# A 32-batch GRU recurrence on one core: in its last five steps, r and h_n are laid ahead of z, and z goes to a bank of its own

## The chip, the cores and the metric

The kernel runs on one core of a Trainium2 chip. The metric is the device time of one execution in microseconds; less is better. Engines: PE (TensorE) multiplies matrices into PSUM, ACT (ScalarE) applies functions, DVE (VectorE) does elementwise work, reductions and 32x32 transpositions, POOL (GpSimd) does little here, and SP (SyncE) issues the DMAs.

## What is computed

A GRU with batch B = 32, T = 64 steps and D = 512 runs over `x`, then a block attention with a layer norm over its output. All values are float32. Cut to what matters here:

```
def cell(h, x):                       # 64 times, each on the h of the one before
    i_r, i_z, i_n = split(x @ W_ih + b_ih)
    h_r, h_z, h_n = split(h @ W_hh + b_hh)
    r = sigmoid(i_r + h_r)
    z = sigmoid(i_z + h_z)
    n = tanh(i_n + r * h_n)
    return (1 - z) * n + z * h
x = x + GRU(x)
# attention over 8 blocks of 8 steps: keys = block sums @ Wk.T, RMS-normed, dotted
# with a query, softmax; attended = weighted block sums; proj = attended @ Wo.T
out = x + layernorm(x + proj) * gamma + beta
```

Step t needs the state of step t-1, so the 64 steps are one chain. z is needed only for the last line of the cell, r and h_n for the tanh.

## The kernel before, in words

**Layout.** State and gates stand in "recurrence layout": partition 32 j + b holds quarter j (128 columns of 512) of batch row b. So each of r, z, n is a tile of 128x128. For h @ W_hh the state is transposed in 32x32 blocks (`turned`), and for each of 4 chunks k of the contraction four matmuls, one for each quarter j, run beside each other on four column strips of the array; each has a stationary tile of 128x32 and moves 384 columns: r, z and h_n of that quarter (L648, 16 matmuls a step; the profile counts 32, two passes each). They add onto what ACT has put into the bank `gates_ps` before: the bias of h_n (`seed_n`, L417) and i_r, i_z (`seed_rz`, L426).

**A step** t = i*8 + s: PE's 16 matmuls (`gates_ready`); ACT's sigmoid over r and z in one instruction of 256 columns (L493); DVE's product r * h_n (L937, `rh_ready`); DVE adds i_n in two parts, 32 and 96 columns (L944); ACT takes tanh of each (L502); DVE forms (z - 1) * n (L862), subtracts it from z * h (L939, L945 make `zh`; L869) and turns the new state (L875) in three parts of 32, 32 and 64 columns; PE's group k = 0 waits for the first part, k = 1 for the second, k = 2 and 3 for the third (`ht_ready`). ACT seeds h_n's columns after L937 and those of r and z after the tanhs.

**Between the steps** each engine runs other work in program order, behind its part of the step. Up to step 58 PE computes x @ W_ih for later steps (L616). In the last five steps, t = 59 to 63 (s = 3 to 7 of the last block), that has run out. PE has there: two of four key matmuls of 512 columns in each of steps 59 to 62 (L630; `keys(0, ..)` in 59 and 60, `keys(1, ..)` in 61 and 62), a mask matmul behind them in step 59 (L658), the first four blocks' scores in step 61 (L662), the tokens' sums of squares in step 62 (L670). ACT has `add_beta` (L453), `centre_wo` (L471), `square_keys` (L433), which waits for the keys, the statistics of a token tile (L439, L442) and `move_s2` (L479). DVE has the sum x + h in transposed layout (L881, step 59), after which SP sends the state out as `h_tok` (L257, 4 DMAs), token centring (L898), the keys' dot products, the early scores (L1036, L1038, step 60) and the early attention (L1050, L1054, step 61). In steps with t % 4 = 0 the write of the state's first part (L869) also waits for the `h_tok` DMAs of the four steps before.

**Step 63** uses whole tiles: the sigmoid (L488), r * h_n (L1063), tanh (L490), `zh` (L1066) and so on, then the last block sum (L1123), from which the last keys and their projection start (L736), and the layer norm. `first_ps`, the bank of step 0, is free from step 4 on until the tail, where `lay_x1` writes it (L729, `out_ps[0]`).

The order of every engine's instructions is written out by hand, with semaphores.

Of the kernel before, what the change touches and what calls it, by code (L numbers as in the profile page):

```python
# [13 lines left out]
P = 128  # L14
# [10 lines left out]
def gru_block_attention(nc, x_tok_d, x_t_d, cond_d, w_ih_d, w_hh_d, bias_d, recs_d, rows_d, wk_t_d,  # L25
# [3 lines left out]
    with ctx:  # L29
# [104 lines left out]
        rz_ready, n_ready, rh_ready = sem("rz_ready"), sem("n_ready"), sem("rh_ready")  # L134
        terms_ready, h_ready = sem("terms_ready"), sem("h_ready")
# [57 lines left out]
        def gates_bank(t):  # L193

            return first_ps[t] if isinstance(t, int) and t < Q else gates_ps

# [189 lines left out]
        def _(act):  # L386
# [32 lines left out]
            def seed_rz(i, s, t):  # L419

                if s % Q == 0:

                    for c in range(2):
                        wait(act, gi_moved[c], (i * 2 + s // Q) * 32)
                first = (s % Q) * G3
                act.activation(gates_ps[:, P:3 * P], gi[:, (s // Q) % 2, first + P:first + G3], ACT.Copy  # L426
                               ).then_inc(seeded, 1)

# [54 lines left out]
            def step(i, s, peeled=False, last=False):  # L483
                t = i * S + s

                if last and s == S - 1:
                    act.wait_ge(gates_ready, T)
                    act.activation(rz[:], gates_ps[:, P:3 * P], ACT.Sigmoid).then_inc(rz_ready, 1)  # L488
# [3 lines left out]
                wait(act, gates_ready, t + 1)  # L492
                act.activation(rz[:], gates_bank(t)[:, P:3 * P], ACT.Sigmoid).then_inc(rz_ready, 1)  # L493
                seeds = not (isinstance(t, int) and t < Q - 1)
                if seeds:

                    wait(act, rh_ready, t + 1)
                    seed_n()
                for number, c in enumerate((slice(0, B), slice(B, P))):
# [96 lines left out]
        def _(pe):  # L596
# [38 lines left out]
            def step(i, s, first=False, last=False):  # L635
# [5 lines left out]
                for k in range(NJ):  # L641
# [5 lines left out]
                    for j in range(NJ):  # L647
                        mm = pe.matmul(gates_bank(t)[j * B:(j + 1) * B, P:], before[:, k * B:(k + 1) * B],  # L648
                                       chunk(w_hh, k, j), start=False, stop=(k == NJ - 1), skip_group_check=True)
# [101 lines left out]
            pe.wait_ge(beta_added, NQ)  # L751
            lay_x1(0)
# [89 lines left out]
        def _(dve):  # L842
# [86 lines left out]
            def step(i, s, peeled=False, last=False):  # L929
# [9 lines left out]
                dve.tensor_tensor(zh[:, first], z[:, first], before[:, first], ALU.mult).then_inc(terms_ready, 1)  # L939
# [5 lines left out]
                dve.tensor_tensor(zh[:, rest], z[:, rest], before[:, rest], ALU.mult).then_inc(terms_ready, 1)  # L945
# [112 lines left out]
            def last_step():  # L1058
# [6 lines left out]
                dve.tensor_tensor(n[:], r, gi[:, 1, (Q - 1) * G3:(Q - 1) * G3 + P], ALU.add).then_inc(n_pre_ready[0], 1)  # L1065
                dve.tensor_tensor(zh[:], z, hist[:, S - 2, :], ALU.mult).then_inc(terms_ready, 1)  # L1066
# [235 lines left out]
```

## Time and profile before

| | us |
|---|---|
| median of 3 runs (367.89 to 368.25) | 368.22 |
| the profiled execution, its whole time | 368.15 |
| its span in the profile | 366.30 |
| PE busy in the span | 358.6 |
| DVE busy | 263.6 |
| ACT busy | 166.4 |

The whole time and the span differ by the 1.85 us that lie around the span. Times in a timeline are microseconds from the span's start; a duration runs from an instruction's start to its end, and neighbours on one engine may overlap, since the next one begins while the last drains. In a merged row (x4, x32) the duration is that of the whole group. PE's ends are modelled.

### The profile page before, as it was taken

The numbers are of one execution on the slowest core, as the hardware profiler recorded it, in microseconds if no ns is written. First come the engines' busy times: TensorE is split into PE (matmuls) and PEld (weight loads), VectorE is DVE, ScalarE is ACT, GpSimd is POOL, SyncE is SP. The second block draws the span as 40 slices with busy tenths as digits, with TensorE's granted clock in tenths as the row PEclk, the third lists the DMA queues.
The fourth block names the chain that finished last, engine by engine and source line by source line (L and its number), as shares of the span: only waits on it lengthen the run. The fifth ranks groups of instructions, "written<-read, shape, count | busy, mean of one in ns | idle before, by whom it ended". The sixth has DMA issues, their size and how long they took to land.

```text
span 366.3 us, 9562 instructions
## 1 busy us (share of the span) xinstructions
PE 358.6 (98%) x3096; PEld 185.4 (51%) x3096; DVE 263.6 (72%) x1129; ACT 166.4 (45%) x525; POOL 11.7 (3%) x46
## 2 busy tenths in 40 slices
PE   8999999999999999999999999999999999999995
PEld 4545555444555544555544555544555544434772
DVE  3827767677777767776768767776867676888886
ACT  4852236252625343442626262534445255857430
POOL 6000000000000000000000000000000000000000
PEclk9999999999999999999999999999999999999999
DMA  7952625323232322223132323232222312211138
GB/s 309 420 185 73 195 93 166 91 64 88 86 86 86 86 72 72 86 60 112 43 100 57 86 86 86 84 88 64 77 88 57 111 42 69 71 29 30 31 140 320
DMA packets 36275, 38.35 MB, mean 105 GB/s; under 512 B 3992, under 2 KB 27672, under 8 KB 36256
## 3 DMA queue, kind: packets, MB, share of 16 engines
q1 hardware_dynamic: 36240, 38.09, 33.5%
q8 instruction: 11, 0.18, 0.2%
q14 instruction: 8, 0.07, 0.1%
q10 hardware_dynamic: 16, 0.02, 0.0%
HBM read 17.91 MB, written 4.19 MB: 60 GB/s over the span
## 4 chain that ended last, share of the span: by engine, by line
PE 86%; DMA 5%; DVE 3%; issue 3%; SPq 1%; ACT 0%; DVEq 0%; POOLq 0%; POOL 0%; ACTq 0%
PE gates_ps L648 43%; PE gi_ps L616 36%; DMA w_hh<-in_w_hh_dram 2%; DMA gcx<-in_w_ih_dram 2%; PE gi_ps L630 1%; PE fourth_ps L648 1%; PE third_ps L648 1%; PE keys_ps L648 1%; DMA h_tok<-hist 1%; PE gi_ps L729 1%; DVE gcx L1226 0%; PE small_ps L795 0%; SPq L283 0%; DVEq L29 0%; PE small_ps L729 0%
## 5 line engine op out<-in xcount | busy, mean ns | idle before, releaser
L648 PE MATMUL gates_ps<-w_hh,turned 128*32 128x384 f32 x1920 | 167.3, 489 | 0.4 <-DVE turned L875 0.3
L648 PEld LDWEIGHTS gates_ps<-w_hh,turned 128*32 128x32 f32 x1920 | 56.4, 109 | 90.5 <-issue 48.8
L493 ACT ACTIVATE rz<-gates_ps 128x256 f32<-128x256 f32 x59 | 22.7, 384 | 129.1 <-PE gates_ps L648 129.1
L616 PE MATMUL gi_ps<-w_ih_hi,xt_hi 128*128 128x512 f32 x180 | 76.4, 427 | 0.0
L616 PE MATMUL gi_ps<-w_ih_lo,xt_hi 128*128 128x512 f32 x180 | 70.5, 394 | 0.0
L616 PE MATMUL gi_ps<-w_ih_hi,xt_lo 128*128 128x512 f32 x180 | 69.5, 389 | 0.0
L937 DVE TENSOR_TENSOR rz<-gates_ps,rz 128x128 f32<-128x128 f32 x59 | 17.2, 291 | 72.1 <-ACT rz L493 72.0
L616 PEld LDWEIGHTS gi_ps<-w_ih_hi,xt_hi 128*128 128x128 f32 x180 | 33.6, 187 | 42.3 <-issue 36.8
L616 PEld LDWEIGHTS gi_ps<-w_ih_hi,xt_lo 128*128 128x128 f32 x180 | 33.8, 188 | 7.7
L875 DVE STREAM_TRANSPOSE turned<-hist 128x32 f32<-128x32 f32 x189 | 36.1, 216 | 2.1
L616 PEld LDWEIGHTS gi_ps<-w_ih_lo,xt_hi 128*128 128x128 f32 x180 | 33.8, 188 | 5.4 <-issue 0.6
L869 DVE TENSOR_TENSOR hist<-zh,n 128x32 f32<-128x32 f32 x189 | 33.6, 201 | 2.5 <-DVE n L862 0.2
L854 DVE TENSOR_TENSOR gi_tok<-gi_ps,b_in 128x512 f32<-128x512 f32 x45 | 30.7, 683 | 0.0
L862 DVE SCALAR_TENSOR_TENSOR n<-rz,n 128x32 f32<-128x32 f32 x189 | 30.4, 188 | 0.0
L502 ACT ACTIVATE n<-n 128x32 f32<-128x32 f32 x126 | 28.5, 257 | 2.2 <-DVE n L944 1.7
L417 ACT ACTIVATE gates_ps<-bhh_n 128x128 f32<-128x128 f32 x60 | 16.9, 282 | 21.4 <-DVE rz L937 21.4
L426 ACT ACTIVATE gates_ps<-gi 128x256 f32<-128x256 f32 x60 | 22.2, 370 | 0.0
L944 DVE TENSOR_TENSOR n<-rz,gi 128x32 f32<-128x32 f32 x118 | 21.3, 222 | 0.4
L453 ACT ACTIVATE x1t<-x1t,beta_t (+1 forms) x64 | 20.2, 386 | 0.0
L881 DVE TENSOR_TENSOR x1t<-x1t,turned 128x512 f32 (+1 forms) x15 | 16.5, 1103 | 1.9
L945 DVE TENSOR_TENSOR zh<-rz,hist 128x96 f32<-128x96 f32 x63 | 15.8, 251 | 0.0
L391 ACT ACTIVATE xt_hi<-x1t 128x512 fp32r (+1 forms) x15 | 9.4, 629 | 9.0 <-PE gi_ps L616 9.0
(232 smaller groups left out, 295.8 us busy)
## 6 DMA issues: line engine op xcount, KB each, us to landing
gi<-gi_tok SPq DMA_DIRECT2D x60, 128.0 KB, 3.0
x1t<-in_x_t_dram SPq DMA_DIRECT2D x16, 256.0 KB, 2.7
gcx<-in_x_tok_dram SPq DMA_DIRECT2D x16, 256.0 KB, 2.8
h_tok<-hist SPq DMA_DIRECT2D x64, 64.0 KB, 2.1
out_dram<-gcx SPq DMA_DIRECT2D x16, 256.0 KB, 2.1
gi<-gi_tok SPq DMA_DIRECT2D x60, 64.0 KB, 2.2
gcx<-in_w_ih_dram SPq DMA_DIRECT2D x4, 768.0 KB, 6.7
w_hh<-in_w_hh_dram SPq DMA_DIRECT2D x4, 768.0 KB, 9.4
```

What stands on the lines that cost most here:

```text
L426: act.activation(gates_ps[:, P:3 * P], gi[:, (s // Q) % 2, first + P:first + G3], ACT.Copy).then_inc(seeded, 1)
L453: ins = act.activation(tile[:, k, :], tile[:, k, :], ACT.Identity, bias=beta_t[:, k * B:k * B + 1])
L493: act.activation(rz[:], gates_bank(t)[:, P:3 * P], ACT.Sigmoid).then_inc(rz_ready, 1)
L502: act.activation(n[:, c], n[:, c], ACT.Tanh).then_inc(n_ready, 1)
L616: mm = pe.matmul(gi_ps[tok][:], a[:, k, :], chunk_cols(w[:, k, :], c), start=(m % 12 == 0), stop=(m % 12 == 11))
L648: mm = pe.matmul(gates_bank(t)[j * B:(j + 1) * B, P:], before[:, k * B:(k + 1) * B], chunk(w_hh, k, j), start=False, stop=(k == NJ - 1), s ...
L854: dve.tensor_tensor(chunk_rows(gi_tok[:, tok, :], c), chunk_rows(gi_ps[tok][:], c), chunk_cols(b_in[:], c), ALU.add).then_inc(gi_tok_ready, 1)
L862: dve.scalar_tensor_tensor(out=n[:, c], in0=z[:, c], scalar=1.0, in1=n[:, c], op0=ALU.subtract, op1=ALU.mult).then_inc(terms_ready, 1)
L869: dve.tensor_tensor(hist[:, s, c], zh[:, c], n[:, c], ALU.subtract).then_inc(h_ready, 1)
L875: dve.transpose(turned[:, s, c], hist[:, s, c]).then_inc(ht_ready, 1)
L937: dve.tensor_tensor(r, bank[:, 3 * P:], r, ALU.mult).then_inc(rh_ready, 1)
L944: dve.tensor_tensor(n[:, c], r[:, c], i_n[:, c], ALU.add).then_inc(n_pre_ready[number], 1)
```

## The change

For t = 59 to 63 (`z_apart`), PE's 16 matmuls are split in two sets of 16: first r and h_n (256 columns in two runs of 128, into `gates_ps`, whose z columns stay unused), which signal `rn_laid`; then, after a wait for z's seed, z (128 columns, into columns 256 to 383 of `first_ps`). ACT takes r's sigmoid on `rn_laid`, seeds h_n, then takes z's sigmoid on `gates_ready`, before the tanhs; it seeds r and z in two instructions in place of one. DVE drops the two parts of `zh` for one of 128 columns, which waits for z's sigmoid and stands behind the two additions of i_n. In the tail PE waits for the last z before it writes `first_ps`.

```diff
--- before.py
+++ after.py
@@ -132,6 +132,7 @@
         gates_ready, ht_ready, seeded = sem("gates_ready"), sem("ht_ready"), sem("seeded")
         n_pre_ready = [sem("n_pre_ready0"), sem("n_pre_ready1")]
         rz_ready, n_ready, rh_ready = sem("rz_ready"), sem("n_ready"), sem("rh_ready")
+        rn_laid, z_ready, z_seeded = sem("rn_laid"), sem("z_ready"), sem("z_seeded")
         terms_ready, h_ready = sem("terms_ready"), sem("h_ready")
         x1t_ready, part_ready, beta_added = sem("x1t_ready"), sem("part_ready"), sem("beta_added")
         x1t_part_ready = sem("x1t_part_ready")
@@ -194,6 +195,12 @@
 
             return first_ps[t] if isinstance(t, int) and t < Q else gates_ps
 
+        z_ps = first_ps[0][:, 2 * P:3 * P]
+
+        def z_apart(t):
+
+            return isinstance(t, int) and t >= T - 5
+
         def by_step(tile):
 
             return tile.rearrange("p (c t) -> p c t", t=Q)
@@ -423,8 +430,24 @@
                     for c in range(2):
                         wait(act, gi_moved[c], (i * 2 + s // Q) * 32)
                 first = (s % Q) * G3
+                if z_apart(t):
+                    act.activation(gates_ps[:, P:2 * P], gi[:, (s // Q) % 2, first + P:first + 2 * P], ACT.Copy
+                                   ).then_inc(seeded, 1)
+                    wait(act, z_ready, t - (T - 5))
+                    act.activation(z_ps, gi[:, (s // Q) % 2, first + 2 * P:first + G3], ACT.Copy).then_inc(z_seeded, 1)
+                    return
                 act.activation(gates_ps[:, P:3 * P], gi[:, (s // Q) % 2, first + P:first + G3], ACT.Copy
                                ).then_inc(seeded, 1)
+
+            def sigmoid_r(t):
+
+                act.wait_ge(rn_laid, t - (T - 5) + 1)
+                act.activation(r, gates_ps[:, P:2 * P], ACT.Sigmoid).then_inc(rz_ready, 1)
+
+            def sigmoid_z(t):
+
+                act.wait_ge(gates_ready, t + 1)
+                act.activation(z, z_ps, ACT.Sigmoid).then_inc(z_ready, 1)
 
             def square_keys(group):
 
@@ -484,18 +507,23 @@
                 t = i * S + s
 
                 if last and s == S - 1:
-                    act.wait_ge(gates_ready, T)
-                    act.activation(rz[:], gates_ps[:, P:3 * P], ACT.Sigmoid).then_inc(rz_ready, 1)
+                    sigmoid_r(t)
+                    sigmoid_z(t)
                     act.wait_ge(n_pre_ready[0], T)
                     act.activation(n[:], n[:], ACT.Tanh).then_inc(n_ready, 1)
                     return
-                wait(act, gates_ready, t + 1)
-                act.activation(rz[:], gates_bank(t)[:, P:3 * P], ACT.Sigmoid).then_inc(rz_ready, 1)
+                if z_apart(t):
+                    sigmoid_r(t)
+                else:
+                    wait(act, gates_ready, t + 1)
+                    act.activation(rz[:], gates_bank(t)[:, P:3 * P], ACT.Sigmoid).then_inc(rz_ready, 1)
                 seeds = not (isinstance(t, int) and t < Q - 1)
                 if seeds:
 
                     wait(act, rh_ready, t + 1)
                     seed_n()
+                if z_apart(t):
+                    sigmoid_z(t)
                 for number, c in enumerate((slice(0, B), slice(B, P))):
 
                     wait(act, n_pre_ready[number], t + 1)
@@ -645,8 +673,21 @@
                     if first and s == 0:
                         pe.wait_ge(w_hh_in[k], 16)
                     for j in range(NJ):
-                        mm = pe.matmul(gates_bank(t)[j * B:(j + 1) * B, P:], before[:, k * B:(k + 1) * B],
-                                       chunk(w_hh, k, j), start=False, stop=(k == NJ - 1), skip_group_check=True)
+                        rows = slice(j * B, (j + 1) * B)
+                        if z_apart(t):
+                            mm = pe.matmul(gates_ps[rows, P:].rearrange("p (g c) -> p g c", g=3)[:, 0::2],
+                                           before[:, k * B:(k + 1) * B], chunk(w_hh, k, j)[:, 0::2],
+                                           start=False, stop=(k == NJ - 1), skip_group_check=True)
+                        else:
+                            mm = pe.matmul(gates_bank(t)[rows, P:], before[:, k * B:(k + 1) * B], chunk(w_hh, k, j),
+                                           start=False, stop=(k == NJ - 1), skip_group_check=True)
+                if z_apart(t):
+                    mm.then_inc(rn_laid, 1)
+                    pe.wait_ge(z_seeded, t - (T - 5) + 1)
+                    for k in range(NJ):
+                        for j in range(NJ):
+                            mm = pe.matmul(z_ps[j * B:(j + 1) * B, :], before[:, k * B:(k + 1) * B], chunk(w_hh, k, j)[:, 1],
+                                           start=False, stop=(k == NJ - 1), skip_group_check=True)
                 mm.then_inc(gates_ready, 1)
                 if not (last and s >= Q - 1):
                     q = (s + 1) // Q + 1
@@ -749,6 +790,7 @@
                       start=True, stop=True).then_inc(scores_ps_ready, 1)
             pe.wait_ge(s2_moved, 1)
             pe.wait_ge(beta_added, NQ)
+            pe.wait_ge(z_ready, 5)
             lay_x1(0)
             lay_x1(1)
             keep_warm_again(2)
@@ -936,13 +978,18 @@
                 i_n = bank[:, 0:P] if bank is not gates_ps else gi[:, slot, tt * G3:tt * G3 + P]
                 dve.tensor_tensor(r, bank[:, 3 * P:], r, ALU.mult).then_inc(rh_ready, 1)
                 before = hist[:, (s - 1) % S, :]
-                dve.tensor_tensor(zh[:, first], z[:, first], before[:, first], ALU.mult).then_inc(terms_ready, 1)
+                if not z_apart(t):
+                    dve.tensor_tensor(zh[:, first], z[:, first], before[:, first], ALU.mult).then_inc(terms_ready, 1)
                 wait(dve, rh_ready, t + 1)
                 if tt == 0 and bank is gates_ps:
                     wait(dve, gi_moved[2], quad * 64)
                 for number, c in enumerate((first, rest)):
                     dve.tensor_tensor(n[:, c], r[:, c], i_n[:, c], ALU.add).then_inc(n_pre_ready[number], 1)
-                dve.tensor_tensor(zh[:, rest], z[:, rest], before[:, rest], ALU.mult).then_inc(terms_ready, 1)
+                if z_apart(t):
+                    dve.wait_ge(z_ready, t - (T - 5) + 1)
+                    dve.tensor_tensor(zh[:], z, before, ALU.mult).then_inc(terms_ready, 2)
+                else:
+                    dve.tensor_tensor(zh[:, rest], z[:, rest], before[:, rest], ALU.mult).then_inc(terms_ready, 1)
 
                 wait(dve, n_ready, t * 2 + 1)
                 take_n(0)
@@ -1063,6 +1110,7 @@
                 dve.tensor_tensor(r, gates_ps[:, 3 * P:], r, ALU.mult).then_inc(rh_ready, 1)
                 dve.wait_ge(rh_ready, T)
                 dve.tensor_tensor(n[:], r, gi[:, 1, (Q - 1) * G3:(Q - 1) * G3 + P], ALU.add).then_inc(n_pre_ready[0], 1)
+                dve.wait_ge(z_ready, 5)
                 dve.tensor_tensor(zh[:], z, hist[:, S - 2, :], ALU.mult).then_inc(terms_ready, 1)
                 dve.wait_ge(scores_ps_ready, 1)
                 dve.tensor_reduce(neg_max, fourth_ps[:, 0:NB - 1], AX.X, ALU.max, negate=True
```

PE, in steps 59 and 60 (`gates_ps` takes r and h_n, `first_ps` z, `gi_ps` the keys, `small_ps` the mask). Before:

```order
L648 MATMUL gates_ps<-w_hh,turned 32x384 x16
L630 MATMUL gi_ps<-wk_t,br_t 128x512 x2
L658 MATMUL small_ps<-same_b,tok_of_b 128x128
L648 MATMUL gates_ps<-w_hh,turned 32x384 x16
L630 MATMUL gi_ps<-wk_t,br_t 128x512 x2
```

Now:

```order
L678 MATMUL gates_ps<-w_hh,turned 32x2x128 x16
L689 MATMUL first_ps<-w_hh,turned 32x128 x16
L658 MATMUL gi_ps<-wk_t,br_t 128x512 x2
L699 MATMUL small_ps<-same_b,tok_of_b 128x128
L678 MATMUL gates_ps<-w_hh,turned 32x2x128 x16
L689 MATMUL first_ps<-w_hh,turned 32x128 x16
L658 MATMUL gi_ps<-wk_t,br_t 128x512 x2
```

The 16 matmuls of 384 columns became 16 of 256 and 16 of 128; keys and mask stand behind both sets.

ACT, in step 61 (`rz` holds the two sigmoids, `n` the tanh). Before:

```order
L493 ACTIVATE rz<-gates_ps 128x256
L417 ACTIVATE gates_ps<-bhh_n 128x128
L502 ACTIVATE n<-n 128x32
L502 ACTIVATE n<-n 128x96
L426 ACTIVATE gates_ps<-gi 128x256
L453 ACTIVATE x1t<-x1t,beta_t 128x128 x4
```

Now:

```order
L445 ACTIVATE rz<-gates_ps 128x128
L424 ACTIVATE gates_ps<-bhh_n 128x128
L450 ACTIVATE rz<-first_ps 128x128
L530 ACTIVATE n<-n 128x32
L530 ACTIVATE n<-n 128x96
L434 ACTIVATE gates_ps<-gi 128x128
L437 ACTIVATE first_ps<-gi 128x128
L476 ACTIVATE x1t<-x1t,beta_t 128x128 x4
```

z's sigmoid moved between the seed of h_n and the first tanh, and the seeding takes two instructions.

DVE, in step 61, up to the first part of the new state. Before:

```order
L937 TENSOR_TENSOR rz<-gates_ps,rz 128x128
L939 TENSOR_TENSOR zh<-rz,hist 128x32
L944 TENSOR_TENSOR n<-rz,gi 128x32
L944 TENSOR_TENSOR n<-rz,gi 128x96
L945 TENSOR_TENSOR zh<-rz,hist 128x96
L862 SCALAR_TENSOR_TENSOR n<-rz,n 128x32
```

Now:

```order
L979 TENSOR_TENSOR rz<-gates_ps,rz 128x128
L987 TENSOR_TENSOR n<-rz,gi 128x32
L987 TENSOR_TENSOR n<-rz,gi 128x96
L990 TENSOR_TENSOR zh<-rz,hist 128x128
L904 SCALAR_TENSOR_TENSOR n<-rz,n 128x32
```

z * h is one instruction, behind both additions and right ahead of (z - 1) * n.

## Rows read from the trace of the kernel before

**Rows 1.** Page, costliest groups: line engine op out<-in xcount | busy, mean ns | idle.

```profile
L648 PEld LDWEIGHTS gates_ps<-w_hh,turned 128*32 128x32 f32 x1920 | 56.4, 109 | 90.5 <-issue 48.8
L426 ACT ACTIVATE gates_ps<-gi 128x256 f32<-128x256 f32 x60 | 22.2, 370 | 0.0
```

**Rows 2.** Timeline of PE, steps 59 to 63: start us, us, engine line op.

```profile
317.91 0.48 PE L658 MATMUL small_ps<-same_b,tok_of_b 32*128 32x128 f32 x2
318.32 2.79 PE L648 MATMUL gates_ps<-w_hh,turned 128*32 128x384 f32 x32
...
323.29 2.79 PE L648 MATMUL gates_ps<-w_hh,turned 128*32 128x384 f32 x32 [0.26 <-DVE turned L875]
326.01 1.96 PE L630 MATMUL gi_ps<-wk_t,br_t 128*96 128x512 f32 x4
327.80 0.28 PE L662 MATMUL keys_ps<-b_in,same_b 128*128 128x4 f32 x2
328.18 2.79 PE L648 MATMUL gates_ps<-w_hh,turned 128*32 128x384 f32 x32
...
332.69 0.32 PE L670 MATMUL small_ps<-b_in 128*128 128x48 f32 x2
333.06 2.79 PE L648 MATMUL gates_ps<-w_hh,turned 128*32 128x384 f32 x32
...
338.66 1.08 PE L736 MATMUL keys_ps<-wk_t,br_turned 128*32 128x128 f32 x32 [0.60 <-DVE br_turned L1123]
339.56 1.06 PE L736 MATMUL gates_ps<-wo_t,br_turned 128*32 128x128 f32 x32
```

**Rows 3.** The chain of waits, steps 59 and 60: start us, us, what.

```profile
318.81 1.12 DVE x1t L881
...
320.60 2.12 DMA h_tok<-hist
322.71 0.19 DVE hist L869
```

**Rows 4.** Timeline of DVE, steps 59 to 63.

```profile
316.55 0.29 DVE L937 TENSOR_TENSOR rz<-gates_ps,rz 128x128 f32<-128x128 f32 x1 [0.91 <-ACT rz L493]
...
320.92 0.21 DVE L1082 TENSOR_TENSOR b_in<-s_tok,b_in 128x48 f32<-128x48 f32 x1
...
326.07 0.23 DVE L1038 TENSOR_SCALAR b_in<-own_n,b_in 128x4 f32<-128x4 f32 x1
326.55 0.29 DVE L937 TENSOR_TENSOR rz<-gates_ps,rz 128x128 f32<-128x128 f32 x1 [0.24 <-ACT rz L493]
...
327.36 0.19 DVE L862 SCALAR_TENSOR_TENSOR n<-rz,n 128x32 f32<-128x32 f32 x1
...
331.05 0.35 DVE L1054 SCALAR_TENSOR_TENSOR b_in<-br_all,b_in 128x128 f32<-128x128 f32 x1
...
336.06 0.17 DVE L926 TENSOR_TENSOR b_in<-b_in,own_n 128x8 f32<-128x8 f32 x1
336.32 0.29 DVE L1063 TENSOR_TENSOR rz<-gates_ps,rz 128x128 f32<-128x128 f32 x1
```

**Rows 5.** Timeline of ACT, steps 59 to 63.

```profile
315.10 0.71 ACT L471 ACTIVATE wo_t<-wo_t,wo_sum 128x512 f32<-128x512 f32 x1
...
326.87 0.28 ACT L417 ACTIVATE gates_ps<-bhh_n 128x128 f32<-128x128 f32 x1 [0.36 <-DVE rz L937]
327.10 0.23 ACT L502 ACTIVATE n<-n 128x32 f32<-128x32 f32 x1
...
332.89 0.57 ACT L433 ACTIVATE third_ps<-gi_ps 96x512 f32<-96x512 f32 x1 [0.17 <-PE gi_ps L630]
...
335.61 0.17 ACT L479 ACTIVATE b_in<-small_ps 32x12 f32<-32x12 f32 x1
335.90 0.38 ACT L488 ACTIVATE rz<-gates_ps 128x256 f32<-128x256 f32 x1
```

**Rows 6.** Timeline of PE's weight loads, step 61.

```profile
323.78 0.31 PEld L648 LDWEIGHTS gates_ps<-w_hh,turned 128*32 128x32 f32 x8 [0.34 <-DVE turned L875]
```

## The prediction

> **What bounds the kernel now.** I read the timelines of PE, DVE and ACT over the last five steps, then the chain of waits there, then single rows beside them. I write P60 to P63 for the start of a step's gate matmuls (the rows of PE that say gates_ps), R for the start of DVE's r * h_n, and N for the start of (z - 1) * n on the first 32 columns. P60 to P63 are 318.32, 323.29, 328.18 and 333.06 [rows 2], so a step takes 4.9 to 5.0 us.
>
> One step reads so, on step 61: PE runs from 323.29 for 2.79; r * h_n starts at R = 326.55, that is P + 3.26, right behind the sigmoid; N is 327.36, R + 0.81; the next step's PE starts at 328.18, N + 0.82 [rows 2, 4]. That is the recurrence's chain. But PE is filled too. The keys start 2.72 after P and last 1.96, and L662 behind them ends at 328.08, 0.10 before P62 [rows 2]. In step 59 the mask ends at 318.39 and P60 is 318.32 [rows 2]: PE is the bound there, and PE's next step can begin 0.07 before the modelled end. So PE could start step 62 at 328.01 at the earliest, and step 63 at 332.94 (L670 ends at 333.01): 0.17 and 0.12 before it does. A faster chain gains no more than that in those steps.
>
> Step 60 is bound by something else: the chain of waits goes from L881 on DVE (318.81) by the send of `h_tok` (DMA from 320.60 for 2.12) to the state's write at 322.71 [rows 3]. That write waits for the DMA, whatever r and z do. And step 63's sigmoid starts at 335.90, behind `move_s2` on ACT, whose last piece runs from 335.61 for 0.17 [rows 5]. That series on ACT began at 332.89 with `square_keys`, released by PE's last keys [rows 5]: what step 63 gains hangs on when PE ends its keys in step 62.
>
> **The parts, each against the rows.**
>
> *PE, r and h_n first.* L736 shows matmuls on the same four column strips with 128 columns: the next 32 start 0.90 later, and their own 1.08 shows a tail of 0.18 [rows 2]. So 384 columns stream in 2.79 - 0.18 = 2.61, or 0.87 per 128 columns. r and h_n: 1.74; z: 0.87 by this, 0.90 by L736. I add d = 0.03 a step to PE for the split. r's sigmoid can start at P + 1.74 + 0.18 + 0.05 = P + 1.97, where the one sigmoid starts at P + 2.84 now (R less 0.42; the 0.38 of L488 and a 0.04 hop [rows 5]). A sigmoid of 128 columns is not in the trace as such; the nearest is the seed of the same size, 0.28 [rows 5], so R = sigmoid + 0.32. Ends: 0.28 and 0.38. Together R could come at P + 2.29, 0.97 earlier, if ACT and DVE are free.
>
> *PE waits for the turned state sooner.* Group k = 0 now takes 1.74 / 4 = 0.43 in place of 0.65, but the load of group k = 1 came at 323.78, released by the second transposition [rows 6], so its matmul at about P + 0.53. Where the chain is the bound, PE stalls 0.10. Ends: 0 (the state early) and 0.10.
>
> *ACT, z behind h_n's seed.* The seed starts at R + 0.32 and the tanh 0.23 behind it [rows 4, 5]. z's sigmoid takes that place, and the tanh moves to R + 0.78. DVE's z * h waits for z: R + 0.55 + 0.28 + 0.04 = R + 0.87. N can start some 0.20 behind it, at R + 1.07, in place of R + 0.81. So each step pays **0.26** after R. The extra seed instruction: two of 0.28, spaced 0.23, for one of 0.37 [rows 1, 5], whose next started 0.30 behind it: 0.16 later for what follows on ACT. PE's new wait for z's seed costs nothing: ACT writes it right behind the tanhs of the step before, over 2 us ahead of its use. The tail's new wait for z is covered too, since z's last sigmoid ends about 336.25, before PE has the scores, which need L926 (336.06 plus 0.17) [rows 4].
>
> **The sum, step by step.**
>
> - Step 59. ACT is still in `centre_wo`, ending at 315.81 and now 0.16 later [rows 5]. An instruction can start 0.05 before its predecessor ends, so r's sigmoid starts at 315.92 and R is 316.24, 0.31 earlier than 316.55 [rows 4]. Less 0.26: N, L881 and the DMA behind it gain **0.05**. P60 is PE's: + 0.03.
> - Step 60. r would allow R at 320.61; DVE is in L1082 (320.92, now 0.05 earlier) and is free some 0.12 behind its start: R = 320.99. N = 322.06, but the state's write waits for the DMA at 322.66. P61 = 323.24.
> - Step 61. r allows R at 325.63; DVE's L1038 starts at 326.07 - 0.05, so R is 326.14, and 0.41 of gain shrinks to 0.15 at N = 327.21. The chain gives P62 = 328.03. PE gives 328.01 - 0.05 + 0.10 (stall) + 0.03 = 328.09. P62 is 328.09, **0.09** earlier; PE took the rest.
> - Step 62. L1054 starts at 331.05 - 0.15, with 0.27 to the next: R = 331.17, N = 332.24, P63 = 333.06, unchanged. But the keys follow P62, not P63: they end 0.09 - 0.03 = 0.06 earlier, and so does ACT's series.
> - Step 63. `move_s2` lets ACT go at 335.67, r was laid at 335.1; R could be 335.99. DVE's L926 starts at 336.00 and is over in 0.12 to 0.17: R = 336.14, against 336.32 [rows 4]. From there on the whole-tile step is as before, since z's sigmoid fits before the tanh: **-0.18** at the end.
>
> 368.15 (the profiled execution, 366.30 of it span) less 0.2 is 367.95. The median stands 0.07 above that execution, so I forecast **368.0**. A measurement of this kernel can tell 0.2%, 0.74 us, from no change; this is a fifth of it.
>
> **Rivals.**
>
> *A: the fillers give way* and the chain sets the pace. Then P + 1.97 + 0.10 + 0.32 + 1.07 + 0.82 = P + 4.28 against 4.89 in steps 60 to 62, 0.6 a step; over four steps and the end 2.4 to 3, which gives **365.3**. For it: the chain is what the trace names at P61, P62 and P63. Against: PE has 4.79 us of its own work in step 61, a DMA ends step 60, and DVE's fillers hold R in steps 60 to 62. Winning in one step alone would give 367.4.
>
> *B: R does not move.* If r's sigmoid starts no earlier, because ACT or DVE are busier than I read, only the 0.26 stays: at step 59 (to P61), at step 61 (to P62), with d twice: + 0.6, **368.8**. It decides where R gains less than 0.26; my least gain is 0.31, in step 59. Against it: 0.41 in step 61.
>
> *C: z's weight loads come out from under the matmuls* (slower). A step has 32 loads, 56.4 / 60 = 0.94 us of busy time [rows 1], hidden under 384 columns now. Under z's 128 columns they may not be. Wholly bare they add 0.94 to PE in each of steps 59 to 62. P60 pays it whole; P61 pays some 0.6, since in step 60 PE is done at P + 2.72 + 1.96 - 0.07 = 322.93 and has 0.3 to spare; steps 61 and 62 pay 0.8 and 0.9. In all + 2.3, **370.5**. It decides for "slower" when the split costs over 0.3 a step. Against it: L736 does just this with 128 columns, at 0.90 for 32 [rows 2], 0.03 above the streaming time.
>
> A rule of the Trainium skill speaks for C. "TensorE: Matmul & The Clock Gate", section on the back-to-back issue gap, gives about 81 ns for each matmul of N = 128 in a sustained stream of load and matmul pairs. By it z's 32 would take 2.6 us, 1.7 more a step, and the time would be an estimated 374. The 0.90 for 32 disagrees: 28 ns each, on four column strips side by side; I go by the row.
>
> **How the numbers follow.** My forecast 0.77, all of it within 0.2%; A 0.12, faster; B 0.05, still within 0.2%; C 0.06, slower. So faster 0.12, same 0.82, slower 0.06. The range starts at A's one-step case, 367.4, and ends at B, 368.8. The unknown costs lie inside it: a sigmoid of 0.38 puts R 0.10 later in a few steps, a stall of 0 brings P62 0.10 forward. Left out are most of A and C, under 0.2.
>
> **What would show it.** In the profile after: r's sigmoid starting near P + 2.0 in steps 60 and 61, near 315.9 in step 59 and 335.7 in step 63; DVE without idle time before r * h_n in steps 60 to 62 (0.24 in step 61 before); tanh 0.78 behind R; the state's write in step 60 still released by the DMA, near 322.66; P62 near 328.1, with PE's own work ending just before; gates of 1.74 + 0.90 on PE. Wrong: P61 before 323.0 or after 323.4, PE's two sets together over 2.8, or R63 off 336.14 by more than 0.3.

## The result, and the profile after

The kernel after takes **369.1 us** (median of 17 runs, 368.27 to 369.8) against 368.25 us before (17 runs, 367.81 to 370.69). The ratio is 1.0022, 95% interval 1.0013 to 1.0030: slower by 0.8 us, where 368.0 and "no change" stood in the prediction. The profiled execution took 369.1 us with a span of 367.3; before it was 368.15 and 366.3.

The five steps are not where the time went. PE's timeline of the kernel after, steps 59 to 63 (start us, us, engine line op):

```profile
318.43 1.93 PE L678 MATMUL gates_ps<-w_hh,turned 128*32 128x256 f32 x32
320.18 1.06 PE L689 MATMUL first_ps<-w_hh,turned 128*32 128x128 f32 x32
321.17 1.98 PE L658 MATMUL gi_ps<-wk_t,br_t 128*128 128x512 f32 x4
323.08 1.93 PE L678 MATMUL gates_ps<-w_hh,turned 128*32 128x256 f32 x32
...
328.25 2.00 PE L678 MATMUL gates_ps<-w_hh,turned 128*32 128x256 f32 x32 [0.35 <-DVE turned L917]
...
333.30 2.00 PE L678 MATMUL gates_ps<-w_hh,turned 128*32 128x256 f32 x32
...
338.63 1.08 PE L777 MATMUL keys_ps<-wk_t,br_turned 128*32 128x128 f32 x32 [0.41 <-DVE br_turned L1171]
```

From P60 to the last keys it is 20.20 us (318.43 to 338.63), before 20.34 (318.32 to 338.66 [rows 2]): 0.14 less, where the prediction had 0.2. The last layer norm follows unchanged. DVE's last instruction starts at 363.09 before and 363.05 after:

```profile
363.05 0.74 DVE L1274 SCALAR_TENSOR_TENSOR gcx<-gcx,w_hh,gi_ps 128x512 f32<-128x512 f32 x1
```

What comes behind it is the end of the output stores. The issues on SP, single rows of the timeline; before:

```profile
357.08 0.34 SPq L327 DMA_DIRECT2D out_dram<-gcx  x1
357.74 0.34 SPq L327 DMA_DIRECT2D out_dram<-gcx  x1
359.02 0.34 SPq L327 DMA_DIRECT2D out_dram<-gcx  x1
```

and after:

```profile
357.04 0.34 SPq L334 DMA_DIRECT2D out_dram<-gcx  x1
357.70 1.76 SPq L334 DMA_DIRECT2D out_dram<-gcx  x1
359.50 0.43 SPq L334 DMA_DIRECT2D out_dram<-gcx  x1
359.98 0.45 SPq L334 DMA_DIRECT2D out_dram<-gcx  x1
```

One issue takes 1.76 us in place of 0.34, and the next stand ready behind it. The stretches of the tail (us; busy time with count of PE, PEld, DVE, ACT, POOL; PEclk, DMA share, GB/s), before:

```profile
357.00:359.00 2.00, 2.00 (x17) 1.17 (x16) 1.46 (x4) 0.00 (x0) 0.00 (x0) 1.00 1.02 378
359.00:361.00 2.00, 2.00 (x13) 1.12 (x12) 2.00 (x4) 0.00 (x0) 0.00 (x0) 1.00 0.77 288
361.00:363.00 2.00, 1.33 (x7) 0.34 (x5) 1.87 (x3) 0.00 (x0) 0.00 (x0) 1.00 1.00 380
365.00:366.00 1.00, 0.00 (x0) 0.00 (x0) 0.00 (x0) 0.00 (x0) 0.00 (x0) 1.00 0.43 164
```

and after:

```profile
357.00:359.00 2.00, 2.00 (x17) 1.16 (x16) 1.46 (x4) 0.00 (x0) 0.00 (x0) 1.00 0.84 301
359.00:361.00 2.00, 2.00 (x14) 1.16 (x12) 2.00 (x4) 0.00 (x0) 0.00 (x0) 1.00 0.56 206
361.00:363.00 2.00, 1.29 (x7) 0.30 (x4) 1.87 (x3) 0.00 (x0) 0.00 (x0) 1.00 1.03 383
365.00:366.00 1.00, 0.00 (x0) 0.00 (x0) 0.00 (x0) 0.00 (x0) 0.00 (x0) 0.50 1.03 393
366.30:366.50 0.20, 0.00 (x0) 0.00 (x0) 0.00 (x0) 0.00 (x0) 0.00 (x0) 0.50 0.05 20
```

From 361 the DMA engines are full in both, so what was not moved between 357 and 361 is made up only at the end. The last packet ends at 365.56 before and at 366.54 after: 0.98 us. (The PEclk of 0.50 does no harm there; PE has nothing left to do.)

The page shows what else is new. Its part on busy time and its part on queues, of the kernel after:

```profile
PE 358.9 (98%) x3256; PEld 189.5 (52%) x3256; DVE 263.1 (72%) x1125; ACT 166.8 (45%) x535; POOL 12.0 (3%) x46
...
q8 instruction: 13, 0.21, 0.3%
```

Before, PE had x3096 and the queue `q8 instruction: 11, 0.18, 0.2%`. The split makes 160 matmuls and 160 loads more, and the chip fetched two more blocks of instructions for them. The trace's DMA records list the packets of that queue one by one, 16,384 bytes each, roughly one for 256 of PE's records. The last ones of the two kernels (start us, us, PE's records still to come):

```
before  342.5 1.00 475   349.7 0.88 197
after   341.2 0.93 542   348.0 1.21 295   357.4 1.72  55
```

One block that before did not need falls at 357.4 to 359.1, and the held issue ends at 359.46, 0.37 behind it. On blocks the Trainium skill ("Runtime: NRT & Kernel Launch", section "Instruction fetch mechanics") says that each engine's sequencer fetches its instructions in 16 KiB blocks of 256 on a DMA queue of its own, and that this is mostly hidden. The size and the spacing agree with the records here. "Hidden" is true of PE in this kernel, whose own rows show no stall; the question is whether it is true of the stores.

### The profile page after: what moved, and what is told of

Read it like the earlier page. It is cut to its first block, busy times and chain, and to the rows that moved or that the text cites. A ratio compares the mean times of both kernels' runs of the same rounds, so it can differ in the third digit from the quotient of the medians.

```text
span 367.3 us, 9892 instructions
## 1 busy us (share of the span) xinstructions
PE 358.9 (98%) x3256; PEld 189.5 (52%) x3256; DVE 263.1 (72%) x1125; ACT 166.8 (45%) x535; POOL 12.0 (3%) x46
## 4 chain that ended last, share of the span: by engine, by line
PE 90%; DVE 4%; issue 3%; DMA 1%; ACT 1%; DVEq 0%; POOL 0%; POOLq 0%; ACTq 0%
PE gates_ps L682 41%; PE gi_ps L644 37%; PE gi_ps L658 1%; PE gates_ps L678 1%; DMA gcx<-in_bias_dram 1%; PE first_ps L740 1%; PE fourth_ps L682 1%; PE third_ps L682 1%; PE keys_ps L682 1%; PE first_ps L682 1%; PE fourth_ps L740 1%; PE third_ps L740 1%; PE keys_ps L740 1%; DVE gcx L1274 1%; PE fourth_ps L728 0%
## 5 line engine op out<-in xcount | busy, mean ns | idle before, releaser
L682 PE MATMUL gates_ps<-w_hh,turned 128*32 128x384 f32 x1760 | 153.4, 489 | 0.0
L682 PEld LDWEIGHTS gates_ps<-w_hh,turned 128*32 128x32 f32 x1760 | 51.2, 109 | 83.2 <-issue 44.6
L519 ACT ACTIVATE rz<-gates_ps 128x256 f32<-128x256 f32 x55 | 21.2, 385 | 125.0 <-PE gates_ps L682 125.0
L917 DVE STREAM_TRANSPOSE turned<-hist 128x32 f32<-128x32 f32 x189 | 36.1, 216 | 2.1
L439 ACT ACTIVATE gates_ps<-gi 128x256 f32<-128x256 f32 x55 | 20.3, 370 | 0.0
L992 DVE TENSOR_TENSOR zh<-rz,hist 128x96 f32<-128x96 f32 x59 | 14.8, 251 | 0.0
```

Source lines behind the costliest of these rows:

```text
L682: mm = pe.matmul(gates_bank(t)[rows, P:], before[:, k * B:(k + 1) * B], chunk(w_hh, k, j), start=False, stop=(k == NJ - 1), skip_group_che ...
L917: dve.transpose(turned[:, s, c], hist[:, s, c]).then_inc(ht_ready, 1)
```

## The experiments

Theory F: that block, among stores that fill the DMA engines, costs the time. Theory S: the split of the steps costs it. Theory D: the transfers of the kernel after are slower for a reason of their own. (The expectations, written early, put the block at 357.1; it starts at 357.37.) To compare profiled executions I read two lengths, each from one profiled execution of a kernel: **section**, from P60 to the start of DVE's last instruction, which holds what the split does to steps 60 to 63; and **tail**, from there to the end of the last DMA packet. What the split does to step 59 lies ahead of the section: from its gates to P60 it is 5.07 after and 5.05 before, 0.02. All twelve kernels, with before and after (records: PE's, matmuls alone; block: PE's last instruction block, start and us; held: the longest issue of a store near it):

```
kernel            records  block         held  section  tail  ratio  [95%]
before            3096     349.7 0.88    -     44.76    2.47  1
after             3256     357.4 1.72    1.76  44.62    3.49  1.0022 [1.0013, 1.0030]
before_pad        3153     356.7 0.94    0.42  44.77    2.48  1.0031 [1.0019, 1.0043]
after_pad         3313     352.2 0.98    1.14  44.64    2.47  1.0017 [1.0000, 1.0034]
after_pad_tail    3285     355.3 0.96    0.44  44.62    2.47  1.0007 [0.9988, 1.0026]
split4            3224     351.7 1.06    0.47  44.62    2.47  0.9987 [0.9977, 0.9996]
before_fetch      3124     357.5 1.39    1.67  44.76    3.42  1.0041 [1.0021, 1.0060]
before_fetch28    3138     356.3 1.01    0.60  44.77    2.48  1.0005 [0.9994, 1.0017]
after_2q          3256     357.0 1.44    0.37  44.63    3.26  1.0012 [0.9999, 1.0026]
before_2q         3096     350.1 1.02    0.37  44.76    2.48  0.9996 [0.9982, 1.0010]
split59_62        3224     350.2 0.95    0.48  44.88    2.49  1.0003 [0.9987, 1.0020]
split4_pool       3224     349.5 1.45    0.85  44.20    2.48  0.9996 [0.9986, 1.0006]
before_pool       3096     350.4 0.88    0.35  44.95    2.48  1.0010 [0.9997, 1.0022]
split4_late_sums  3224     348.7 0.93    0.35  44.28    2.48  0.9975 [0.9959, 0.9992]
```

The tail falls into two groups: 3.26 to 3.49 in the three kernels whose last block starts 1.65 to 1.9 us behind the issue of the fifth store (355.72 in the kernel after), the first of the long run of stores, and 2.47 to 2.49 in all others, where the block starts 0.1 to 0.3 ahead of that issue (before_pad, after_pad_tail, before_fetch28) or microseconds earlier. The section depends on the split alone. It is the start of the program (P60 lies between 318.0 and 320.4) and the runs' own scatter that blur the ratios. (split4's profiled execution, at 370.1, was the slowest of its twelve runs: its P60 is the 320.4.)

### Moving the block: padding

`keep_warm` and `keep_warm_again` are matmuls that PE does while it waits. In before_pad and after_pad one of each is replaced by many small ones:

```diff
-            keep_warm(3)
+            for _ in range(31):
+                pe.matmul(gates_ps[0:B, 0:B], xt_hi[:, 0, 0:B], xt_hi[:, 0, 0:B], start=True, stop=True)
...
-            keep_warm_again(2)
+            for _ in range(31):
+                pe.matmul(keys_ps[0:B, 0:B], xt_hi[:, 0, 0:B], w_ih_hi[:, 0, 0:B], start=True, stop=True)
```

before_pad:

> The kernel before, with its gates untouched, but about 114 more PE instructions ahead of the tail: 31 tiny matmuls (32 columns, no result used) in place of three warm-up matmuls at the start, and 31 in place of two keep-warm matmuls behind lay_x1(1). Theory F (fetch): PE's program is fetched in blocks of 16 KB, one per about 256 PE records; in the changed kernel one more block comes at 357.1, for 1.72 us, while SP issues the stores, whose eighth takes 1.76 us in place of 0.34, and that costs about 1 us. Here the same last block falls about 55 records before PE's end too, so theory F expects it near 357, a held-up store, and 0.7 to 1.1 us more than before, about 369.1. Theory S (split): the loss comes from the five split steps; expects 368.1 to 368.5 (the padding itself 0 to 0.3). Theory D (the stores' transfers are slower in the changed kernel for reasons of their own): expects 368.1 to 368.5.

after_pad:

> The changed kernel with the same 114 or so additional PE instructions in the same two places. Theory F: the last block of PE's program is then fetched near 350 to 352, ahead of the stores' dense phase, no store is held, and the time falls to 367.9 to 368.4. Theory S and theory D: the split and the stores are as in the changed kernel, so 369.0 to 369.4, perhaps 0.3 more for the padding.

after_pad_tail has the second edit alone:

> The changed kernel with only the padding behind lay_x1(1), about 58 more PE instructions. Theory F: the last block comes some 2 to 4 us earlier than 357.1, near 353 to 355, where SP waits for DVE between the fourth store (352.1) and the fifth (355.7): 367.9 to 368.5, unless the block still holds a store. Theories S and D: 369.0 to 369.4.

after_pad: the block moved to 352.2, and held a store there too (1.14 us), which cost nothing, since the queue stood idle until 356.7 anyway; the tail is back at 2.47. Its median is 369.34 all the same, inside what S and D forecast (369.0 to 369.4 and perhaps 0.3 more); in its profile P60 is at 319.40, 0.97 later. after_pad_tail has no padding at the start: 368.56, the tail 2.47. Both bear F out, the first by its profile only. before_pad **missed**: it was to show a held store, and its 369.38 looks like one, but the block came at 356.7, 0.24 ahead of the fifth store (356.93), took 0.94 and held an issue for 0.42 at most, and the whole loss is P60 at 319.49. That the padding at the start moved P60 is likely but not shown by the profiles alone, where P60 is as late as 320.4 without it; for it speaks that all six runs of before_pad lie at 369.21 or above. A median alone would have misled.

### The split in four steps

```diff
-            return isinstance(t, int) and t >= T - 5
+            return isinstance(t, int) and t >= T - 4
```

> The change in the last four steps only (steps 60 to 63), 64 PE records fewer than the changed kernel. Theory F: PE's end now comes ahead of the block boundary (55 records before the end in the changed kernel), so no block is fetched during the stores: 367.9 to 368.3. Theory S: four fifths of the loss stay, 368.9. Theory D: 369.0.

368.0, ratio 0.9987 (0.9977 to 0.9996): 32 matmuls fewer, the last block already at 351.7 with the first stores, where it cost nothing (tail 2.47), and the change is no loss but a small gain. Its section, 44.62, is that of the kernel after, 0.14 to 0.15 shorter than before's; that much of the gain has its rows.

### The block without the split

before_fetch is the kernel before, with three `keep_warm_again` of the tail made of 6, 15 and 12 small matmuls; nothing at the start and nothing in the recurrence changes. before_fetch28 has 10, 22 and 15.

> The kernel before, gates untouched, start untouched; in the tail five keep-warm matmuls of 512 columns are replaced by 6, 15 and 12 tiny ones (32 columns, result unused), 56 PE records more in about the same PE time. By the block positions seen so far, this puts the last block of PE's program where the changed kernel has it, near 357. Theory F (that fetch holds a store): 0.7 to 1.1 us more than before, 369.1, with one store of SP held over 1 us and the last transfers ending as much later, while DVE's last instruction stands where it did (363.1). Theory S (the split steps) and theory D (the changed kernel's transfers are slower by themselves): same as before, 368.1 to 368.5.

> As the run before it, with 10, 22 and 15 tiny matmuls, 84 PE records more than the kernel before, so the last block should come near 356, about a microsecond sooner. Theory F: it depends on what the block meets; if a store is issued while it is in flight and held until it lands, then as long as the block takes: 0.1 to 0.4 us of hold if it takes 0.9 to 1.0, with no loss in time, since fewer transfers are pending there; 368.2 to 369.0. Theories S and D: 368.1 to 368.5.

before_fetch reproduces the loss: 369.57, ratio 1.0041 (1.0021 to 1.0060). That is somewhat more than forecast; its profiled execution, at 368.93, shows 0.95 of it, all in the tail (3.42), with DVE's last instruction no later than before (362.92). Its issues on SP:

```profile
356.91 0.34 SPq L327 DMA_DIRECT2D out_dram<-gcx  x1
357.57 1.67 SPq L327 DMA_DIRECT2D out_dram<-gcx  x1
359.28 0.43 SPq L327 DMA_DIRECT2D out_dram<-gcx  x1
```

and its stretches:

```profile
357.00:359.00 2.00, 2.00 (x18) 1.07 (x18) 1.46 (x3) 0.00 (x0) 0.00 (x0) 1.00 0.78 282
359.00:361.00 2.00, 2.00 (x13) 1.11 (x12) 2.00 (x4) 0.00 (x0) 0.00 (x0) 1.00 0.67 247
365.00:366.00 1.00, 0.00 (x0) 0.00 (x0) 0.00 (x0) 0.00 (x0) 0.00 (x0) 0.50 0.94 354
```

The rows are those of the kernel after, without one line of its change. With 14 matmuls more, before_fetch28 has its block at 356.3, 0.13 ahead of its fifth store, and its stores are issued in 0.60 and 0.42 (357.06, 357.71): tail 2.48, 368.38. So the same block costs 1 us or nothing, by where it falls, and without any split: theories S and D are out for this microsecond of the tail.

### What the block holds: two queues

```diff
-            for quad in range(NQ):
+            for quad in [quad for quad in range(NQ) if quad < 7 or quad % 2 == 0]:
...
+            for quad in range(7, NQ, 2):
+
+                act.wait_ge(out_ready, quad + 1)
+                act.dma_start(out[:, quad, :], gcx[:, quad, :]).then_inc(out_stored_act, 16)
```

after_2q:

> The kernel after, with the stores of five of the sixteen quads (7, 9, 11, 13, 15) issued by ACT and the rest by SP; PE's instructions are as after. Theory F (a block of PE's instructions is fetched among the output stores and one store's issue on SP is held behind it for 1.4 us): if it holds only SP's issue, ACT's stores go on beside it and the 1.0 us shrinks, 368.1 to 368.6. If the block takes the DMA engines' time itself, or holds both queues, it stays near 369.1. Theory S (the split of the last five steps costs the time, stores or not): 369.1, with no stretched issue needed for it. Either way I expect the trace to show the block near 357.5 on the page's axis of after.

before_2q, the control:

> Control: the same five stores issued by ACT in the kernel before, which has no held store. Theory F: 368.0 to 368.5, no difference beyond the measurement, since the transfers and not the issues fill the last 8 us. If the second queue by itself gained over 0.3 us here, then a gain of the other run would say nothing of the fetch.

after_2q: 368.95, ratio 1.0012 (0.9999 to 1.0026). No issue was held this time, neither ACT's at 357.32 (0.37, as long as the same issue took in before_2q with no block near) nor SP's at 358.60 (0.34, begun behind the block's end), and yet the tail is 3.26. before_2q: 368.44, ratio 0.9996 (0.9982 to 1.0010), tail 2.48, so the second queue alone changes nothing. F's first form, that all of the loss hangs on SP's held issue, **missed**. The stretches say why:

```profile
359.00:361.00 2.00, 2.00 (x14) 1.07 (x12) 2.00 (x4) 0.00 (x0) 0.00 (x0) 1.00 0.81 301
...
364.00:365.00 1.00, 0.00 (x0) 0.00 (x0) 0.00 (x0) 0.00 (x0) 0.00 (x0) 1.00 1.00 375
365.00:365.20 0.20, 0.00 (x0) 0.00 (x0) 0.00 (x0) 0.00 (x0) 0.00 (x0) 1.00 0.21 72
365.20:365.90 0.70, 0.00 (x0) 0.00 (x0) 0.00 (x0) 0.00 (x0) 0.00 (x0) 1.00 0.06 23
```

For the last 0.7 us the share is 0.06, one engine of sixteen: fifteen are done by 365.20 and one goes on alone to 365.92, a packet of 2,048 bytes every 0.08 us. A block of 16 KB is eight such packets, 0.64 us of one engine. That this is the engine that carried the block is an inference, since the records do not name engines; but in the profiles with a tail of 2.5 the last twenty packets of the stores end within 0.16 us of each other.

So the block can cost in two ways, and they overlap. Without a held issue (after_2q) fifteen engines end 2.5 behind DVE's last instruction, as before, and the lone one costs 0.8. With it, in the kernel after, the hold leaves all engines nearly idle for over a microsecond:

```profile
358.50:359.00 0.50, 0.50 (x7) 0.42 (x4) 0.50 (x2) 0.00 (x0) 0.00 (x0) 1.00 0.24 90
359.00:359.50 0.50, 0.50 (x4) 0.30 (x4) 0.50 (x1) 0.00 (x0) 0.00 (x0) 1.00 0.06 8
...
366.20:366.30 0.10, 0.00 (x0) 0.00 (x0) 0.00 (x0) 0.00 (x0) 0.00 (x0) 0.50 0.13 41
```

All but two are done by 366.20, some 3.2 behind DVE's last instruction where it was 2.47 before, so the hold is worth some 0.7 there; from 366.30 one goes on alone (share 0.05, shown above) to 366.54. Taking the hold away (after_2q) gained only 0.2 of the tail (3.49 to 3.26) and 0.15 of the median. Why the lone engine did not catch up in after_2q while the engines stood nearly idle (share 0.15 from 359.00 to 359.50), I can't tell from these records.

When is an issue held? The timelines of all fourteen kernels answer it better than the stores alone. SP's issues that begin while a PE block is on its way are of two kinds. Where SP's issue before had ended at most 0.4 us earlier (76 of them), each ended 0.32 to 0.43 behind the block's end, however long that took. Where SP had issued nothing for 1.86 us or more (34 of them), none was held: each took what it takes without a block, 0.34 to 0.61. So the first issue behind a pause goes free, and the next ones are held. The blocks at 356.3 and 356.7, right ahead of the fifth store, fit that: the fifth store went free, and little of the block was left for the sixth. It also fits ACT's issue in after_2q, the first on its queue since the start of the program, so that run does not tell whether ACT's queue would have been held like SP's.

### The steps themselves

```diff
-            return isinstance(t, int) and t >= T - 5
+            return isinstance(t, int) and T - 5 <= t < T - 1
```

> The change in steps 59 to 62 alone; step 63 as before, so PE has 64 instruction records fewer than after. Theory F: the last block of PE's instructions then falls among none of the stores, or ahead of them (about 352), and the last DMA ends 2.5 us behind DVE's last instruction: 367.9 to 368.3. Theory S: four fifths of the loss stay, 368.9. Step 63 itself: r * h_n would come no earlier than z and r together, so the section from the gates of step 60 to the turned keys should be 0.0 to 0.1 longer than after's 20.20.

No block in the long run of stores, tail 2.49, as F has it; 368.52, ratio 1.0003, which is above the forecast of 368.3. The section is 44.88, 0.26 more than after's, where I expected 0.1 at most. DVE's timeline of this kernel, step 63:

```profile
336.65 0.29 DVE L1110 TENSOR_TENSOR rz<-gates_ps,rz 128x128 f32<-128x128 f32 x1 [0.17 <-ACT rz L511]
```

R63 is P63 + 3.26 (333.39), as before; with the split it is P63 + 3.01 (336.31 less 333.30). So the split earns its 0.26 in step 63 and loses 0.12 in steps 60 to 62.

Two kernels then tried to let those steps gain, by taking DVE's fillers (its other work between the steps) out of the way of r * h_n. In split4_pool POOL does the early attention sum in three instructions (L389 to L394), and two block sums move behind the states of steps 61 and 62; before_pool has the same without the split.

> The split in steps 60 to 63, and on DVE, whose fillers hold R there, less work ahead of the steps: the early attention's four instructions of 128 columns go to GpSimd (three instructions, same sums in another order), and two block sums move behind the states of steps 61 and 62. If DVE's fillers are what kept the split from paying, as my reading has it, R in step 61 comes 0.4 to 0.5 earlier than in the split4 run, P62 0.3 to 0.4, PE's last keys 0.3 to 0.5: 367.3 to 367.7. If PE's own fillers or something else hold the steps, 367.9 to 368.1, as split4.

> The same move of DVE's fillers, without the split. Before, R follows the sigmoid at P + 3.26 and DVE waits for it in steps 60 and 61, so by my reading nothing is gained: 368.1 to 368.4. If the fillers were the bound without the split too: 367.7 or less.

The section of split4_pool is 0.42 shorter than split4's, that of before_pool 0.18 longer than before's: the fillers bind only with the split, as expected. Both medians **missed**: 368.08 (0.9996, 0.9986 to 1.0006) does not show the gain, where 367.3 to 367.7 was forecast, and before_pool's 368.74 (1.0010, 0.9997 to 1.0022) lies above its 368.1 to 368.4. What the move costs is in the trace; DVE of split4_pool, step 62:

```profile
330.49 0.29 DVE L992 TENSOR_TENSOR rz<-gates_ps,rz 128x128 f32<-128x128 f32 x1 [0.61 <-ACT rz L458]
330.82 0.90 DVE L1000 TENSOR_TENSOR n<-rz,gi 128x32 f32<-128x32 f32 x2
...
331.85 0.44 DVE L917 SCALAR_TENSOR_TENSOR n<-rz,n 128x32 f32<-128x32 f32 x1
```

and POOL:

```profile
330.88 0.72 POOL L392 TENSOR_TENSOR gi<-gi 128x256 f32<-128x256 f32 x1
331.75 0.49 POOL L394 TENSOR_TENSOR b_in<-gi 128x128 f32<-128x128 f32 x1
```

Beside POOL's additions the pair of L1000 takes 0.90 and not 0.36, and L917 0.44 and not 0.19. The last kernel leaves POOL out and only moves two sums, on DVE:

```diff
@@ step 60's tail
-                    dve.wait_ge(pre_step, 1)
-                    dve.wait_ge(part_ready, NQ - 1)
-                    dve.tensor_tensor(last_part, last_part, parts_t[:, 0, :], ALU.add).then_inc(pre_step, 1)
-                    add_to_part(s, 2)
@@ step 62's tail, the same with add_to_part(4, 2)
```

> The change in steps 60 to 63, with DVE's two sums of the last block's partial products taken out of step 60's tail and put behind step 62's state. They stand ahead of r * h_n in step 61. Theory (the fillers on DVE hold r * h_n, the change's gain is behind them): R of step 61 about 0.3 to 0.5 earlier, the gates of step 62 0.1 to 0.3 earlier (PE's own work bounds them), and 0.1 to 0.3 less in all than the same kernel without the move (368.0): 367.7 to 368.0. Rival: the sums cost in step 62's tail what they gave in 60's, ahead of the last steps' attention sums, and the time is 368.0 or above. PE's instructions are as in that kernel, so no store is held.

**367.56, ratio 0.9975 (0.9959 to 0.9992).** It is the fastest of the fourteen, faster than the kernel before and, by the medians, than the kernel after (its ratio is to the kernel before; it was not timed against the kernel after directly). It beat its forecast of 367.7 to 368.0. DVE's timeline:

```profile
324.37 0.68 DVE L928 TENSOR_REDUCE parts_t<-x1t 128x128 f32<-128x512 f32 x1
...
325.32 0.23 DVE L1085 TENSOR_SCALAR b_in<-own_n,b_in 128x4 f32<-128x4 f32 x1
325.46 0.28 DVE L979 TENSOR_TENSOR rz<-gates_ps,rz 128x128 f32<-128x128 f32 x1
...
335.63 0.28 DVE L1110 TENSOR_TENSOR rz<-gates_ps,rz 128x128 f32<-128x128 f32 x1
```

R61 is P60 + 7.35 (318.11) against 7.91 in the kernel after, and the section 44.28, 0.33 less than split4's. The sums cost nothing in step 62's tail, where DVE would have waited for ACT. The median fell by 0.44 from split4's; 0.33 of it has its rows.

## Why the prediction was wrong

**The failed step is one that has no term.** "The sum, step by step" ends with step 63: "From there on the whole-tile step is as before", -0.18 at the end. I counted PE's 160 more matmuls as streaming time (d = 0.03 a step) and never as instructions that have to be fetched. The term left out is +1.0 us, in the stores, some 20 us behind step 63. No rival had it either: B and C price waits and loads inside the steps. The page of the kernel before had the queue `q8 instruction` and its count; I had not asked what moves it.

The time was not lost in the steps, but two of their readings were wrong (steps 60 and 61), and the errors cancelled. The terms that were there:

- **d = 0.03.** r and h_n's set starts at 318.43 and z's at 320.18, 1.75; z's takes 0.99 to the keys, in which lies the change from gates to keys. Gates to keys is 2.74 in all (2.72 in [rows 2]): d was 0.02. Right. Where PE waits for the turned state (steps 62 and 63), r and h_n's set takes 2.00 for 1.93, a stall of 0.07 for the 0.10 assumed.
- **Rival C.** z's 32 matmuls and what follows start within 0.99 us, so their loads stay hidden. The row of L736 was the right one to go by. Its sum was wrong, though: 0.94, 0.6, 0.8 and 0.9 make 3.2 and not 2.3, so its time was 371.5 and not 370.5.
- **R + 0.78 for the tanh, N at R + 1.07.** In step 61 R is 326.34, tanh 327.03 and N 327.44: 0.69 and 1.10. So 0.29 a step, for 0.26.
- **Step 59.** r's sigmoid 315.89 (315.92 forecast), R 316.18 (316.24). Right.
- **Step 60.** R 320.99 and N 322.09 came as forecast, but the wait for the DMA that the step's forecast rests on is not there. The wait ahead of the state's write in step 60 (L950 of the kernel before) asks for the sends of quads 0 to 13, `(quad - 1) * (16 * NJ)` with quad 15; SP issued the last of them at 302.08. The send from 319.95 on is that of quad 14, the four steps just before, and the write does not wait for it (the description of the kernel, with "the four steps before", is one quad off). The kernel after shows it: the write starts at 322.38, and the second of that send's four parts signals its landing from 322.37 to 322.67. The chain of waits had put the write down to the signal that came last ahead of it [rows 3]. The rows around the write, before the change:

```profile
322.41 0.19 DVE L862 SCALAR_TENSOR_TENSOR n<-rz,n 128x32 f32<-128x32 f32 x1
322.70 0.19 DVE L869 TENSOR_TENSOR hist<-zh,n 128x32 f32<-128x32 f32 x1
```

  and after:

```profile
322.09 0.18 DVE L904 SCALAR_TENSOR_TENSOR n<-rz,n 128x32 f32<-128x32 f32 x1
322.38 0.19 DVE L911 TENSOR_TENSOR hist<-zh,n 128x32 f32<-128x32 f32 x1
```

  The write is 0.29 behind N in both. So the recurrence's chain bound step 60 like the others, and the split shortened it: P61 is 4.65 behind P60, before 4.97, for a forecast of 4.89. At 323.08 it is PE's keys that end it (321.17 + 1.98, less the 0.07 by which the next set may begin early).
- **Step 61.** R 326.34 for 326.14. I let DVE's fillers come 0.05 earlier; behind P60 they did not, and the rows say what holds them. The chain of waits of the kernel after:

```profile
321.24 1.93 PE gi_ps L658 x4
323.17 0.02 issue
323.19 0.70 ACT third_ps L456 x2
...
324.02 0.69 DVE b_in L959
...
326.20 0.23 DVE b_in L1085
326.43 0.20 DVE rz L979
```

  The fillers hang on PE's keys of step 60, which the split does not bring forward. L1085 starts 7.77 behind P60, before (L1038) 7.75. So nearly all of the 0.32 that step 60 gained is lost: P62 is 9.82 behind P60, before 9.86.
- **Step 62.** R 331.39 for 331.17; P63 is 14.87 behind P60, before 14.74. The forecast was no change.
- **Step 63.** R is P63 + 3.01 for 3.08 forecast; the gain of the step is 0.25 for 0.18.

The sum of these is -0.14 at the last keys for a forecast of -0.2; the total was read about right, against start times that differ by 0.1 anyway, but in part by luck: step 60 gained 0.32 where 0.08 was forecast, and step 61 gave it back. Rival A's condition, the fillers out of the way, is what the last kernel tried in part: the kernel with two fillers moved takes 0.33 more out of the section.

## What to carry over

Where a change adds instructions to an engine that is near its end while transfers fill the DMA engines, count the instruction blocks too, and look at where the last one falls: here it cost 1.0 us or nothing for a shift of 2 us against the stores, and 14 small matmuls, or a split in one step fewer, decided it. Where a small gain does not show in the median, cut the profile into stretches that the change can reach and stretches that it can't; the loss was in the second kind. A gain on a chain is worth what the fillers beside it leave, and moving two sums behind the chain gave more than the split (0.33 of the section for 0.15). And a releaser that a chain of waits names by a semaphore is worth a look at the value that the program waits for: here it was a send issued 20 us earlier, not the one named.

## What the runs showed of the hardware

- A block of 16,384 bytes of PE's instructions took 0.88 to 1.49 us elsewhere and 1.39 to 1.72 us among the long run of output stores.
- While such a block is on its way, an issue on SP that follows another within 0.4 us ends only 0.32 to 0.43 us behind the block (76 of 76 in the fourteen profiles; up to 1.76 us in place of 0.34 for a store). An issue behind a pause of 1.86 us or more was never held (34 of 34). Whether another engine's queue is held the same way is open.
- Behind a block among stores that fill the engines, the trace shows one DMA engine of sixteen late: 0.7 us at share 0.06 in after_2q. That it is the engine that carried the block is inferred.
- Beside POOL's tensor additions (step 62 of split4_pool), DVE's pair of small additions took 0.90 for 0.36, and its 128x32 product 0.44 for 0.19.
- A matmul set of 384 columns split into 256 and 128, on four column strips, cost 0.02 us in 2.72 up to the keys, and 0.08 to 0.09 in steps 62 and 63, where PE waited for the turned state.
